# A stage that finds slots group by group: the third layer's mix, dispatch and recurrence in one stage

## The reference

```
x = x + s * silu(ffn(xn));   xn = layernorm(x)
```

```
y = real(ifft(fft(u) * fft(kernel)))[:1024] + D * u          # a complex recurrence for each of 128 channels
gates = softmax(xf @ w_router + b_router);  topv, topi = top_k(gates, 2)
pos = cumsum(onehot(topi), axis=0)[...] - 1;  keep = pos < cap     # cap = 1.25 * tokens / 8 = 640
```

## Time and profile before

| | us |
|---|---|
| median of 3 runs (lowest, highest) | 3628.3 (3626.35, 3632.51) |
| the profiled execution: its own time | 3630.93 |
| its span | 3629.2 |
| PE busy (share of the span) | 2859.4 (79%) |
| DVE busy | 2360.4 (65%) |
| ACT busy | 1829.8 (50%) |
| POOL busy | 1515.0 (42%) |

### The profile page before, as it was taken

The page is one execution under the profiler, slowest core; times in us unless marked ns, Lnnn a source line. Parts: engine busy times, 40 slices in busy tenths (PEclk is TensorE's granted clock), DMA queues, the critical chain, the costliest instruction groups (busy, mean ns, idle before and its releaser), DMA issues. The chain is left out here.

```text
span 3629.2 us, 66635 instructions
## 1 busy us (share of the span) xinstructions
PE 2859.4 (79%) x21131; PEld 1281.1 (35%) x21132; DVE 2360.4 (65%) x3384; ACT 1829.8 (50%) x2921; POOL 1515.0 (42%) x1109
## 2 busy tenths in 40 slices
PE   3999999999999967399954599999969911383993
PEld 1333333333333326233323122222236611162771
DVE  5666666666666625688885799999923357134662
ACT  2555555555555530144462399999944450144431
POOL 0889989989989970100000001101016603560000
PEclk9999999999999988599986699999989955696995
DMA  2011111111111115200003322222121123113002
GB/s 82 29 46 41 53 46 40 54 44 42 54 40 45 53 48 209 55 1 1 0 2 100 82 52 52 55 55 53 45 84 45 42 76 115 36 42 86 9 12 63
DMA packets 265382, 189.66 MB, mean 52 GB/s; under 512 B 149056, under 2 KB 210872, under 8 KB 264322
## 3 DMA queue, kind: packets, MB, share of 16 engines
q1 hardware_dynamic: 257154, 174.25, 16.9%
q0 software_dynamic: 8128, 14.18, 1.2%
HBM read 105.28 MB, written 67.62 MB: 48 GB/s over the span
## 5 line engine op out<-in xcount | busy, mean ns | idle before, releaser
L329 POOL TENSOR_TENSOR attn_esum<-attn_esum,attn_prob 128x1024 f32<-128x1024 f32 x384 | 903.1, 2352 | 41.3 <-ACT attn_prob L480 17.8
L540 DVE TENSOR_REDUCE attn_half_max<-attn_peek 128x2 f32<-128x1024 f32 x512 | 627.6, 1226 | 397.7 <-PE attn_peek L380 393.9
L480 ACT ACTIVATE attn_prob<-attn_score 128x1024 f32<-128x1024 f32 x512 | 512.4, 1021 | 297.3 <-PE attn_score L363 297.3
L827 ACT ACTIVATE attn_prob<-attn_score 128x512 f32<-128x512 f32 x1024 | 556.3, 596 | 72.8 <-PE attn_score L777 58.6
L844 DVE TENSOR_REDUCE attn_half_max<-attn_peek 128x2 f32<-128x1024 f32 x512 | 583.7, 1217 | 11.4 <-PE attn_peek L763 11.2
L410 PE MATMUL attn_acc<-attn_prob,attn_v 128*64 128x512 f32 x2048 | 487.9, 597 | 0.1
L793 PE MATMUL attn_acc<-attn_prob,attn_v 128*32 128x256 f32 x4096 | 328.1, 392 | 12.0 <-ACT attn_out L819 10.6
L1755 POOL DMA_INDIRECT sorted_x<-attn_sent_rows,attn_send x64 | 62.6, 978 | 555.6 <-PE attn_score L777 520.3
L763 PE MATMUL attn_peek<-attn_ke,attn_qe 48*128 48x512 bf16 x1024 | 203.0, 394 | 48.0 <-DMA attn_ke<-k 33.3
L380 PE MATMUL attn_peek<-attn_hi 64*128 64x512 f16 x1024 | 200.3, 388 | 44.2 <-DVE attn_half_max L540 44.2
L777 PE MATMUL attn_score<-attn_qe,attn_ke 49*128 49x512 bf16 x1024 | 200.8, 389 | 7.7 <-ACT attn_prob L827 5.8
(11 more groups left out here) (450 smaller groups left out, 4524.4 us busy)
## 6 DMA issues: line engine op xcount, KB each, us to landing
attn_xb<-attn_x_all SPq DMA_DIRECT2D x66, 256.0 KB, 2.5
attn_invB<-inv SPq DMA_DIRECT2D x64, 256.0 KB, 4.0
o<-attn_out SPq DMA_DIRECT2D x32, 512.0 KB, 2.7
out_o<-o SPq DMA_DIRECT2D x8, 2048.0 KB
mix_f<-picked SPq DMA_DIRECT2D x16, 512.0 KB, 7.1
experts_x<-sorted_x SPq DMA_DIRECT2D x112, 65.0 KB
attn_qe<-q SPq DMA_DIRECT2D x192, 32.0 KB
attn_ke<-k SPq DMA_DIRECT2D x192, 32.0 KB
```

The lines of the kernel that those rows point to most:

```text
L329: nc.gpsimd.tensor_tensor(own, before, prob[:, u % NPROB, :, :], ALU.add).then_inc(added, 1)
L480: nc.scalar.activation(prob[:, u % NPROB, :, :], score[:, u % 2, :, :], ACT.Exp).then_inc(exped, 1)
L540: V.tensor_reduce(half_max[:, half, :, t], peek[:], AX.X, ALU.max, negate=True).then_inc(maxed, 1)
L827: nc.scalar.activation(prob[:, n % NPROB, :], score[:, n % RING, :], ACT.Exp).then_inc(exped, 1)
```

## The change

`combine_stage("mix1")`, `dispatch(2, ...)` and `ssm_stage` give way to one stage, `combine_and_send_stage`. Its DVE, ACT and PE lists keep the mix work of `combine_stage` for 4 groups of GT = 8 tiles (first, first_factors, scale_and_shift, combine, second, second_factors have the same instructions; silu now writes over f). Between them stands the slot work of the group before, on 64 columns, with a carry of the counts from group to group: score_group, rank_group, place_group. ACT normalises x straight into `sent_rows`, which has room for both choices, and copies the rows for the second choice. POOL sends the 16 scatters of a group once its slots are there. The clearing stores stand on SP's queue after group 0's loads, and POOL makes the cleared array. The recurrence comes last on DVE, in the space of f and f2. `send` and `pick_weight` no longer pass through DRAM.

```diff
-def ssm_stage(nc, ident, xnT, powers_d, skip, s, beside):
+def combine_and_send_stage(nc, ident, x, s, f_d, f_norm, xnT, w, bias, blocks, xs_d, expert_d, weights, powers_d, skip):
...
+        f, f2 = st.sb("f", [P, NT, D]), st.sb("f2", [P, NT, D])
+        sent_rows = st.sb("sent_rows", [P, 2, NT, ROW])
...
         kept, dd = st.sb("kept", [P, KEPT, SEQ]), st.sb("dd", [P, 1])
...
+        vr, vi, gr, gi = (f[:, n * GT:(n + 1) * GT, :].rearrange("p t d -> p (t d)") for n in range(4))
+        y = f2[:, 0:2 * GT, :].rearrange("p (n t) d -> p n (t d)", n=2)
...
-            job.load(sp)
+            for g in range(NG):
+                for j, dst in enumerate((f, f2)):
+                    sp.dma_start(dst[:, grp(g), :], rows(f_d[j * TOK:(j + 1) * TOK, :])[:, grp(g), :]).then_inc(loaded[g], DMA)
+                if g == 0:
+                    for t, v in zip((gamma, beta), f_norm[:2]):
+                        sp.dma_start(t[:], broadcast_rows(v)).then_inc(consts, DMA)
+                    sp.dma_start(wr[:], w).then_inc(router_in, DMA)
+                    sp.dma_start(bias_b[:], broadcast_rows(bias)).then_inc(router_in, DMA)
+                    sp.wait_ge(zero_made, 2)
+                    for n in range(NZ):
+                        sp.dma_start(xs_d.rearrange("(n p r) d -> n p (r d)", n=NZ, p=P)[n], zero[:].rearrange("p r d -> p (r d)")
+                                     ).then_inc(zeroed, DMA)
             for n in (0, 1, 4, 2, 3):
                 sp.dma_start(kept[:, n, :], powers_d[:, n, :]).then_inc(kept_in[n], DMA)
             sp.dma_start(dd[:], column(skip)).then_inc(skip_in, DMA)
-            job.load_weights(sp)
+            sp.wait_ge(owner_made, 1)
+            sp.dma_start(expert_d[:], owner[:].rearrange("a e b -> a (e b)")).then_inc(owner_stored, DMA)
+            weights.load(sp, weights_in)
+            sp.wait_ge(owner_stored, DMA)
+            sp.wait_ge(weights_in, weights.LOADS * DMA)
...
-            job.run(pool, nc)
+            nc.gpsimd.memset(zero[:], 0.0).then_inc(zero_made, 1)
+            pool.wait_ge(zero_made, 1)
+            nc.gpsimd.iota(zero[:, :, D:D + 1].bitcast(I32), [[0, blocks // NZ], [0, 1]], base=NOWHERE, channel_multiplier=0
+                           ).then_inc(zero_made, 1)
...
+            nc.gpsimd.iota(owner[:], [[1, E], [0, blocks // E]], base=0, channel_multiplier=0).then_inc(owner_made, 1)
+            pool.wait_ge(zeroed, NZ * DMA)
+            for g in range(NG):
+                pool.wait_ge(maps_ready, g + 1)
+                pool.wait_ge(copied, g + 1)
+                for t in range(g * GT, (g + 1) * GT):
+                    for j in range(2):
+                        at = bass.IndirectOffsetOnAxis(ap=send[:, j, t:t + 1].bitcast(U32), axis=0)
+                        pool.indirect_dma_start(out=xs_d[:, :], out_offset=at, in_=sent_rows[:, j, t, :], in_offset=None,
+                                                bounds_check=xs_d.shape[0] - 1, oob_is_err=False).then_inc(sent, DMA)
+            pool.wait_ge(sent, 2 * NT * DMA)
...
+            def score_group(g):
+
+                if g == 0:
+                    dve.wait_ge(router_in, 2 * DMA)
+                dve.wait_ge(logits, g + 1)
+                link(V.tensor_tensor(score[:], lg[:, g % 2, 0:GT * E].rearrange("p (t e) -> p t e", e=E), per_expert(bias_b), ALU.add))
+                link(V.reduce_max(red[:], score[:], AX.X))
+                V.tensor_tensor(shifted[:], score[:], per_tok(red), ALU.subtract).then_inc(shifted_ready, 1)
+
+            def rank_group(g):
+
+                four = [P, GT, E, E]
+                flat = lambda t: t[:].rearrange("p t i j -> p t (i j)")
+                if g == 0:
+                    dve.wait_ge(made, 10)
+                dve.wait_ge(exped, g + 1)
+                link(V.reduce_sum(red[:], score[:], AX.X))
+                link(V.reciprocal(red[:], red[:]))
+                link(V.tensor_tensor(score[:], score[:], per_tok(red), ALU.mult))
+                si, sj = over(score[:].unsqueeze(3), four), score[:].unsqueeze(2).to_broadcast(four)
+                link(V.tensor_tensor(pair2[:], sj, si, ALU.is_equal))
+                link(V.tensor_tensor(flat(pair2), flat(pair2),
+                                     before[:].rearrange("p i j -> p (i j)").unsqueeze(1).to_broadcast([P, GT, E * E]), ALU.mult))
+                link(V.tensor_tensor(pair[:], sj, si, ALU.is_gt))
+                link(V.tensor_tensor(flat(pair), flat(pair), flat(pair2), ALU.add))
+                link(V.reduce_sum(rank[:], pair[:], AX.X))
+                V.tensor_scalar(mask[:], rank[:], 2.0, None, ALU.is_lt).then_inc(mask_ready, 1)
+                for j in range(2):
+                    link(V.tensor_scalar(hot[:, j, :, :], rank[:], float(j), None, ALU.is_equal))
+
+            def place_group(g):
+
+                if g == 0:
+                    link(V.tensor_copy(start[:], start_i[:]))
+                dve.wait_ge(counted, g + 1)
+                link(V.tensor_tensor_scan(upto[:].rearrange("p e t -> p (e t)"), goes_on[:].rearrange("p e t -> p (e t)"),
+                                          tally[:, 1, :], 0.0, ALU.mult, ALU.add))
+                link(V.tensor_tensor(place[:], tally[:, 0, :].rearrange("p (t e) -> p t e", e=E), upto[:].rearrange("p e t -> p t e"), ALU.add))
+                if g:
+                    link(V.tensor_tensor(place[:], place[:], per_expert(carry), ALU.add))
+                    link(V.tensor_tensor(carry[:], carry[:], upto[:, :, GT - 1], ALU.add))
+                else:
+                    link(V.tensor_copy(carry[:], upto[:, :, GT - 1]))
+                link(V.tensor_scalar(keep[:], place[:], float(CAP), None, ALU.is_lt))
+                link(V.tensor_tensor(mask[:], mask[:], keep[:], ALU.mult))
+                link(V.tensor_tensor(place[:], place[:], per_expert(start), ALU.add))
+                link(V.tensor_tensor(each_pick[:], hot[:], both_picks(place), ALU.mult))
+                link(V.reduce_sum(slot[:], each_pick[:], AX.X))
+                link(V.tensor_tensor(each_pick[:], hot[:], both_picks(keep), ALU.mult))
+                link(V.reduce_sum(kept_pick[:], each_pick[:], AX.X))
+                link(V.tensor_scalar(kept_pick[:], kept_pick[:], -FAR, FAR, ALU.mult, ALU.add))
+                link(V.tensor_tensor(send[:, :, grp(g)], kept_pick[:], slot[:], ALU.add))
+                link(V.tensor_tensor(weight[:], mask[:], score[:], ALU.mult))
+                link(V.reduce_sum(red[:], weight[:], AX.X))
+                link(V.tensor_scalar(red[:], red[:], 1e-6, None, ALU.max))
+                link(V.reciprocal(red[:], red[:]))
+                link(V.tensor_tensor(weight[:], weight[:], per_tok(red), ALU.mult))
+                link(V.tensor_tensor(each_pick[:], hot[:], both_picks(weight), ALU.mult))
+                V.reduce_sum(sent_rows[:, :, grp(g), D + 1], each_pick[:], AX.X).then_inc(maps_ready, 1)
...
+            def recur(b):
+                u = xnT[:, b * SEQ:(b + 1) * SEQ]
+                Er, Ei, Wr, Wi, decay = (kept[:, n, :] for n in range(KEPT))
                 if b == 0:
+                    dve.wait_ge(evacuated, NG)
...
+            first(0)
+            first_factors(0)
+            scale_and_shift(0)
+            for g in range(NG):
+                if g + 1 < NG:
+                    first(g + 1)
+                combine(g)
+                if g:
+                    score_group(g - 1)
+                if g + 1 < NG:
+                    first_factors(g + 1)
+                second(g)
+                if g:
+                    rank_group(g - 1)
+                if g + 1 < NG:
+                    scale_and_shift(g + 1)
+                second_factors(g)
+                if g:
+                    place_group(g - 1)
+            score_group(NG - 1)
+            rank_group(NG - 1)
+            place_group(NG - 1)
             for b in range(BATCH):
-                act.wait_ge(turned, b + 1)
-                nc.scalar.activation(s[:, b * SEQ // P:(b + 1) * SEQ // P, :], tp[:, b % 2, :, :], ACT.Copy).then_inc(copied, 1)
+                recur(b)
...
+            mm = nc.tensor.matmul
+            for g in range(NG):
+                pe.wait_ge(xn_ready, g + 1)
+                if g >= 2:
+                    pe.wait_ge(evacuated, g - 1)
+                for t in range(GT):
+                    last = nc.tensor.transpose(tp[:, g % 2, t * P:(t + 1) * P], sent_rows[:, 0, g * GT + t, 0:D], ident[:])
+                last.then_inc(turned, 1)
...
+                pe.wait_ge(evacuated, g + 1)
+                for t in range(GT):
+                    last = mm(lg[:, g % 2, t * E:(t + 1) * E], xnT[:, (g * GT + t) * P:(g * GT + t + 1) * P], wr[:], start=True, stop=True)
+                last.then_inc(logits, 1)
...
+                pe.wait_ge(mask_ready, g + 1)
+                flat = mask[:].rearrange("p t e -> p (t e)")
+                mm(tally[:, 0, :], behind[:], flat, start=True, stop=True)
```

(81 more changed lines are left out.)

127 lines of the change are left out of this document (102 added, 25 removed).

## The result

The changed kernel took 3579.94 us in the median of 4 runs (3575.23 to 3582.55), the kernel before 3629.07 beside it (3626.35 to 3632.51): ratio 0.9863, 95% interval 0.9846 to 0.988. Forecast were 3577, within 3568 to 3592.

The account below looks back on a forecast made before the run. It took a chain of three stages, 226.5 us, ended by POOL's sends, as the bound; DVE's new chain sums to 174.7, saving 51.8: 3579.1 for the profiled execution, 3577 forecast as median, range 3568 to 3592.

Parts of the forecast that it names:

- turn 1: DVE's stretch from group 0's factors to the end of group 0's places: 28.8 to 58.4 us into the stage.
- counting: PE's counting matmuls ahead of places, on 64 columns: between 1.0 and 2.27 us, 1.6 taken; bites at two places.
- the load of group 1: Queued on SP behind the clearing stores: lands at 16.0, DVE asks at 16.2; cost 0, or 2.7 with slow stores.
- the tail: DVE's last stretch before the recurrence, group 3's logits to places with nothing beside the logits: 105.3 to 121.6 us.
- The slack: Last send at 150.9 plus 7.7 us makes 158.6, 16 us before DVE's end, so sends are hidden.
- B: DVE's tensor_scalars wait for the send that runs, up to 17.6 us: 3577 to 3595; chance 0.10.
- C: POOL ends the stage last, from 1.70 us a send; at 2.33 for all, 3617; chance 0.05.
- D: Slower than before: every DVE instruction beside a send is held, tensor_tensors too; 3657; chance 0.03.
- E: Sends go early but the stage's end still waits 7.7 us behind the recurrence, or a load lands late; 3585; chance 0.02.
- A: The stage takes DVE's chain as summed: 3577, own range 3570 to 3584; chance 0.76.

Follow-up runs that it names:

- held sends: The changed kernel, but POOL starts its first send only when the last group's slots are there: 3621.4 us in one run, stage 221.55.
- one wait filled: The changed kernel with one batch of the recurrence run ahead of group 3's scores: 3573.1 us in one run, stage 171.95.
- the recurrence in the gaps: The changed kernel with the recurrence's steps laid into DVE's waits and group 1's loads put first: 3565.82 us, ratio to the kernel before 0.9829, stage 163.25.

## Why the prediction was right

**The bound before, and the whole.** Right: the run with held sends gives back 45 of 50 us, and the runs without sends, with one wait filled and with the loads first leave or move the end as DVE's chain says.

**The steps.** With the stage's start as zero, DVE finished the places of groups 0 to 3 at 60.1, 85.1, 106.8 and 123.3; the prediction had 58.4, 83.5, 105.3 and 121.6. All four are 1.5 to 1.7 late: every turn behind the first had the predicted length within 0.2, and the whole difference arose ahead of the end of turn 1. Within the last two turns the agreement is in part luck: counting cost 1.0 less than was taken, and longer waits for logits (0.7 together) and places of 5.6 and 5.4 for 5.3 gave it back.

**What was mis-sized is the load of group 1:** put at no cost, with 2.7 as its upper bound, it cost 1.35. The prediction set its landing at 16.0 against a need at 16.2, a margin thinner than its two rates were known. The run with the loads ahead, where DVE doesn't wait, shows that the queue did it.

**Waits.** On logits 4.65, 2.93, 4.13 for 4.4, 2.8 and 3.6 (the tail's sum has 3.6, 105.3 to 108.9, where its list of waits says 3.4; 16 matmuls took 3.58, not 3.45); on the exponential 2.56, 2.31, 1.84 for 2.5, 2.6 and 1.8. Counting bit with 0.25 and 0.95, near its lower bound. Small instructions were as taken: 0.23 on 64 elements, 0.29 on 128, 0.69 on 512. The recurrence took 49.1 as forecast.

**Sends.** The first started 0.9 after the places of group 0, a hand-over to POOL that the prediction gave nothing; the last ended 153.5 into the stage, for 150.9. The slack was 15 instead of 16 us, so it cost nothing. The run with the recurrence in the gaps shows what it is worth: the last send and 7.5 us behind it are a bound of their own. What lengthens a send was read too narrowly: the prediction has the trace agree that tensor_tensor leaves sends alone, but a tensor_tensor of 1024 elements makes one 1.83 long in the run with the recurrence in the gaps. In the changed kernel few sends met one so, which the sum could not know.

**The end.** 0.96 from the last copy to the next stage, for 0.8. Sum: 174.7 + 1.35 (load) + 0.3 (turn 1) + 0.16 (end), less 0.1, is 176.4. The profiled execution took 3581.96, for 3579.1 in the sum; the rest of that difference is 1.2 us outside the stage.

**Rivals.** B: beside sends two tensor_scalars of 8 elements took 0.35 and 0.32 instead of 0.17, and a pair on 64 elements 0.56 instead of 0.42; 64 sends removed changed nothing. Of the rule of the Trainium skill ("SBUF — State Buffer", Who interferes with whom), that whichever starts first blocks the other fully, this order of the work showed no more than half a microsecond on DVE's side. That section also says that tensor_tensor with both inputs in SBUF contends with GpSimd's reads, which the prediction left out. The sends' lengths agree with it (last section); which step of a send waits, they don't show. C: 1.45 us a send on average ((153.46 - 60.94)/64, the gaps in it), where 1.70 decides. D came out absent here, but its reason was too weak: the run with the slots behind the loop shows 25 us of held instructions on DVE, with the same sends and the same instructions in another order. What the prediction argued from, the 128x1024 tensor_tensors, says nothing of it, so that this kernel was spared is luck as far as the prediction goes. E: the 7.5 us don't stand behind the recurrence; its late load came, but at 1.35, inside A's range. F: no wait but the counting's was shorter than summed by more than 0.3.

## What to carry to other kernels

Where a long queue of issues on one engine can start only after the last of many small results, hand it the results in blocks; what counts is how early the first block leaves, since the last block and its closing time then slide under other work. Once it is hidden, fill the waits of the engine that now ends last with independent work, and watch for the queue becoming the end again. A load whose landing is summed to within a microsecond of its need should be put first in its queue: it costs nothing, and a stage's first wait shifts all that follows.

## What the runs showed of the hardware

- From the end of the last scatter's issue to the next stage's first instruction 7.54 us pass where the sends end the stage, the same in four runs (7.7 before); from an ACT copy it is 0.96.
- A send takes 0.98 us alone. If a scan or a tensor_tensor of 512 or 1024 elements started on DVE 0.06 us or more before it and runs on for 0.13 or more, the send ends 0.79 us (scan) or 0.86 (tensor_tensor) after that instruction's end. Read off the sends themselves, this fits the length of all 576 in nine runs (this stage and, in the kernel before, "ssm") within 0.04 us: up to 2.80 under a scan (mostly 1.82 to 2.02), 1.02 to 1.95 under a tensor_tensor of 1024, 1.02 to 1.48 under one of 512. DVE's instruction keeps its length. Statistics and reduces, which read one array, don't do it. Beside the recurrence most tensor_tensors ended within 0.12 us of a send's start, which is why they seemed harmless. In the other direction, three tensor_scalars of the changed kernel that started 0.32 to 0.35 us before a send's end ended with it. Below, a pair of the changed kernel, one of the kernel with the recurrence in the gaps, and one of the changed kernel for the other direction:

```profile
3045.03 2.29 DVE L2596 TENSOR_TENSOR_SCAN mix_f<-mix_kept,mix_f 128x1024 f32<-128x1024 f32 x1
3046.09 2.02 POOL L2464 DMA_INDIRECT sorted_x<-mix_sent_rows,mix_send  x1 [0.30 <-issue]
...
2989.06 1.23 DVE L2507 TENSOR_TENSOR mix_f<-mix_f,mix_gamma 128x1024 f32<-128x1024 f32 x1
2989.30 1.83 POOL L2466 DMA_INDIRECT sorted_x<-mix_sent_rows,mix_send  x1 [0.30 <-issue]
...
2985.65 0.98 POOL L2464 DMA_INDIRECT sorted_x<-mix_sent_rows,mix_send  x1 [0.30 <-issue]
2986.28 0.35 DVE L2483 TENSOR_SCALAR mix_var<-mix_moments 128x8 f32<-128x8 f32 x1
```

- Beside a long row of sends DVE can fall to one instruction per 1.40 us for 32 us. The same code ran at full speed without the sends, and with them when 24 instructions had been put ahead (one run each). A kernel whose time jumps by 20 us after a harmless reordering may have this in its timeline: short instructions, each released by its own predecessor, more than a microsecond apart. What causes it stays open.
